# Folding the normalisation's partial sums to 64 rows before the product with ones

## The reference, cut to what matters

```
x = x + 0.5 * ffn(layernorm(x))         # 512 -> 2048 -> 512, weights by their signs, ReLU
x = x + attention(layernorm(x))         # 16 heads of 32
x = x + 0.5 * ffn(layernorm(x))
layernorm(x) = (x - mean(x)) / sqrt(var(x) + 1e-5)      # over the 512 channels
```

## Time and profile before

| | |
|---|---|
| median of 3 runs | 2920.65 us (2915.93 to 2921.74) |
| profiled execution, time | 2917.08 us |
| profiled execution, span | 2915.2 us |
| PE busy | 2864.9 us, 98%, granted clock 0.998 |
| DVE busy | 2049.8 us, 70% |
| ACT busy | 1598.5 us, 55% |
| GpSimd (POOL) busy | 1384.1 us, 47% |

### The profile page before, as it was taken

The page is one execution under the profiler, slowest core; times in us unless marked ns, Lnnn a source line. Parts: engine busy times, 40 slices in busy tenths (PEclk is TensorE's granted clock), DMA queues, the critical chain, the costliest instruction groups (busy, mean ns, idle before and its releaser), DMA issues.

```text
span 2915.2 us, 37959 instructions
## 1 busy us (share of the span) xinstructions
PE 2864.9 (98%) x14288; PEld 1942.2 (67%) x14288; DVE 2049.8 (70%) x3034; ACT 1598.5 (55%) x2847; POOL 1384.1 (47%) x490
## 2 busy tenths in 40 slices
PE   7999999999999999999999999999999999999999
PEld 6888887887755555555555555555555467888887
DVE  5655556768888888888888888888888346555553
ACT  6434434332376766666666666676666653333333
POOL 0000001000089898988888988889888620000000
PEclk9999999999999999999999999999999999999999
DMA  5110102556389999999999999999999852222210
GB/s 188 34 54 29 30 29 66 201 192 191 140 176 189 202 196 202 196 203 194 200 197 202 196 201 195 199 197 204 195 201 209 202 163 58 58 58 58 58 29 29
DMA packets 184375, 424.28 MB, mean 146 GB/s; under 512 B 89728, under 2 KB 90752, under 8 KB 148224
## 3 DMA queue, kind: packets, MB, share of 16 engines
q0 software_dynamic: 31824, 231.75, 38.7%
q1 hardware_dynamic: 152368, 190.11, 23.6%
HBM read 121.91 MB, written 67.63 MB: 65 GB/s over the span
## 4 chain that ended last, share of the span: by engine, by line
PE 90%; DVE 4%; ACT 3%; issue 1%; DMA 1%; POOL 1%; SPq 0%; ACTq 0%; DVEq 0%; POOLq 0%
PE bank L1042 16%; PE bank L1069 16%; PE bank L1038 15%; PE bank L601 15%; PE bank L624 14%; PE bank L751 8%; PE bank L451 3%; ACT att_p L1026 2%; PE bank L1096 1%; POOL att_acc L911 1%; DVE norm_cent L118 1%; ACT head_raw L355 1%; DVE lo L124 0%; PE bank L240 0%; DMA att_dma_acc<-att_p 0%
## 5 line engine op out<-in xcount | busy, mean ns | idle before, releaser
L960 DVE TENSOR_REDUCE att_row_max<-bank 128x1 f32<-128x512 f32 x2048 | 1253.8, 680 | 249.7 <-PE bank L1042 249.6
L1026 ACT ACTIVATE att_p<-bank 128x512 f32<-128x512 f32 x1792 | 910.5, 619 | 399.9 <-PE bank L1038 394.6
L911 POOL TENSOR_TENSOR att_acc<-att_acc,att_p 128x2048 f32<-128x2048 f32 x217 | 1070.8, 4934 | 45.3 <-ACT att_p L1026 41.2
L1042 PE MATMUL bank<-att_k,att_q 96*128 96x512 f32 x2048 | 832.6, 409 | 2.8 <-DVE att_row_max L960 2.6
L1038 PE MATMUL bank<-att_q,att_k 98*128 98x512 f32 x2048 | 818.5, 401 | 9.2 <-ACT att_p L1026 5.3
L1042 PEld LDWEIGHTS bank<-att_k,att_q 96*128 96x128 f32 x2048 | 388.1, 190 | 274.6 <-DVE att_row_max L960 162.1
L1038 PEld LDWEIGHTS bank<-att_q,att_k 98*128 98x128 f32 x2048 | 385.7, 189 | 158.8 <-ACT att_p L1026 44.5
L573 ACT ACTIVATE ffn_hid<-bank,up_s 128x512 f32<-128x512 f32 x256 | 176.2, 688 | 523.1 <-PE bank L601 508.5
L521 DVE TENSOR_TENSOR ffn_hid_lo<-ffn_hid,ffn_hid_hi 128x512 fp32r<-128x512 f32 x256 | 174.6, 687 | 377.8 <-ACT ffn_hid_hi L576 377.8
L1069 PE MATMUL bank<-att_p,att_v 128*32 128x512 f32 x3584 | 439.6, 601 | 0.0
L601 PE MATMUL bank<-hi,ffn_up_w 128*128 128x512 f32 x1024 | 401.1, 392 | 8.9 <-DVE lo L189 4.7
(11 more groups left out here) (117 smaller groups left out, 2390.0 us busy)
## 6 DMA issues: line engine op xcount, KB each, us to landing
att_dma_acc<-att_p POOLq DMA_DIRECT2D x161, 1024.0 KB, 10.3
att_dma_acc<-att_dma_acc POOLq DMA_DIRECT2D x30, 1024.0 KB, 12.6
att_dma_acc<-att_acc POOLq DMA_DIRECT2D x30, 1024.0 KB, 7.4
att_q<-q_hi SPq DMA_DIRECT2D x64, 256.0 KB, 4.0
att_k<-k_hi SPq DMA_DIRECT2D x64, 256.0 KB, 8.1
x<-x_after_ffn SPq DMA_DIRECT2D x15, 1024.0 KB, 7.2
x_after_ffn<-x_out SPq DMA_DIRECT2D x8, 1024.0 KB, 9.5
q_hi<-qkv_o_hi SPq DMA_DIRECT2D x32, 256.0 KB, 2.0
```

The source lines that it names most:

```text
L911: self.nc.gpsimd.tensor_tensor(self.acc[H % 2][:], a[:], self.prob[kt % PR][:], ALU.add).then_inc(self.summed, 1)
L960: self.nc.vector.tensor_reduce(self.row_max[odd][:, qt, q:q + 1], m[:], axis=AX.X, op=ALU.max).then_inc(self.m_read, 1)
L1026: self.nc.scalar.activation(into[:, q * CH:(q + 1) * CH], self.s_ps[(UNITS * H + kt * QC + q) % SR][:], ACT.Exp, scale=SCALE).then_inc(sel ...
L1042: self.nc.tensor.matmul(m[:], self.q_st[T % NB][0:KQ, qt * P:(qt + 1) * P], self.k_st[T % NB][0:KQ, q * CH:(q + 1) * CH], start=True, stop ...
```

## The change

Each statistic's sum is folded once more, from 128 rows to 64, by two further DVE instructions: a copy of rows 64 to 127 of `norm_sum` to rows 0 to 63 of a scratch tile, and an add on 64 rows. Each of the two waits for the instruction before it, through a new semaphore `norm_folding`. The rounded copy of the 64 rows then goes to rows 0 to 63 of one tile `norm_sum_parts`, and what rounding left to rows 64 to 127 of the same tile. PE makes one product of the 128 x 128 matrix of 1/512 with that tile in place of two. The steps, their places in the queues and what PE waits for are as before.

```diff
@@ class Norm, __init__
-        self.sum_hi, self.sum_lo = c.sb("norm_sum_hi", SUM_HI_AT, [P, CH], F32R), c.sb("norm_sum_lo", SUM_LO_AT, [P, CH], F32R)
+        self.parts = c.sb("norm_sum_parts", SUM_HI_AT, [P, CH], F32R)
+        self.folding = c.sem("norm_folding")
@@ centre (the same in square_sums, with 2 * N + 1)
         elif k == 1:
-            ins = nc.vector.tensor_tensor(self.sum[:], self.work[:, 0, :], self.work[:, 1, :], ALU.add)
+            ins = self.fold(dve, 2 * N, 1)
         elif k == 2:
-            ins = nc.vector.tensor_copy(self.sum_hi[:], self.sum[:])
+            ins = self.upper_part()
         elif k == 3:
-            ins = nc.vector.tensor_tensor(self.sum_lo[:], self.sum[:], f32(self.sum_hi[:]), ALU.subtract)
+            ins = self.lower_part()
...
+    def fold(self, dve, which, other):
+        nc, shifted = self.nc, self.work[0:ROWS, 0, :]
+        nc.vector.tensor_tensor(self.sum[:], self.work[:, 0, :], self.work[:, other, :], ALU.add).then_inc(self.folding, 1)
+        dve.wait_ge(self.folding, 2 * which + 1)
+        nc.vector.tensor_copy(shifted, self.sum[ROWS:P, :]).then_inc(self.folding, 1)
+        dve.wait_ge(self.folding, 2 * which + 2)
+        return nc.vector.tensor_tensor(self.sum[0:ROWS, :], self.sum[0:ROWS, :], shifted, ALU.add)
+
+    def upper_part(self):
+        return self.nc.vector.tensor_copy(self.parts[0:ROWS, :], self.sum[0:ROWS, :])
+
+    def lower_part(self):
+        return self.nc.vector.tensor_tensor(self.parts[ROWS:P, :], self.sum[0:ROWS, :], f32(self.parts[0:ROWS, :]), ALU.subtract)
...
@@ vector_first and vector_first_squares: self.fold(dve, 0, 1) and self.fold(dve, 1, 2) in place of the add
@@ tensor
-        nc.tensor.matmul(out[:], self.ones[:], self.sum_hi[:], start=True, stop=False)
-        nc.tensor.matmul(out[:], self.ones[:], self.sum_lo[:], start=False, stop=True).then_inc(self.pe, 1)
+        nc.tensor.matmul(out[:], self.ones[:], self.parts[:], start=True, stop=True).then_inc(self.pe, 1)
```

More of the change, by code:

```diff
@@ L30 @@
 HI1_AT, LO1_AT, X1_AT, CENT_AT, WORK_AT = 128, 136, 144, 152, 160
-SUM_AT, SUM_HI_AT, SUM_LO_AT, VAR_AT = 168, 170, 172, 174
+SUM_AT, SUM_HI_AT, VAR_AT = 168, 170, 174
 HI0_AT, LO0_AT, INV_AT, TMP_AT, HID_AT = 176, 184, 192, 194, 196
@@ L62 @@
 NV, NA = 18, 4
+ROWS = P // 2
 HALF = (slice(0, DT // 2), slice(DT // 2, DT))
@@ L134, in square_sums @@
         if i == 1:
-            ins = nc.vector.tensor_tensor(self.sum[:], self.work[:, 0, :], self.work[:, 1, :], ALU.add)
+            ins = self.fold(dve, 2 * N + 1, 1)
         elif i == 2:
-            ins = nc.vector.tensor_copy(self.sum_hi[:], self.sum[:])
+            ins = self.upper_part()
         elif i == 3:
-            ins = nc.vector.tensor_tensor(self.sum_lo[:], self.sum[:], f32(self.sum_hi[:]), ALU.subtract)
+            ins = self.lower_part()
         ins.then_inc(self.dve, 1)
@@ L179, in vector_first @@
         dve.wait_ge(self.first, 2)
-        nc.vector.tensor_tensor(self.sum[:], work[:, 0, :], work[:, 1, :], ALU.add).then_inc(self.dve, 2)
+        self.fold(dve, 0, 1).then_inc(self.dve, 2)
         for k in (2, 3):
@@ L197, in vector_first_squares @@
         dve.wait_ge(self.first, 6)
-        self.nc.vector.tensor_tensor(self.sum[:], work[:, 0, :], work[:, 2, :], ALU.add).then_inc(self.dve, 2)
+        self.fold(dve, 1, 2).then_inc(self.dve, 2)
         for k in (9, 10):
```

## The result

The kernel after the change takes 2931.4 us (median of 5 runs, 2929.2 to 2935.1) where the kernel before takes 2920.65: ratio 1.0040, with an interval of 1.0028 to 1.0051. So it is slower, by more than the 0.2% that I had set as the bound. I had forecast 2921.0, no measurable change, with 2916 to 2930 as range: direction and range are both missed. Between the medians lie 10.7 us.

A forecast was written before the change was run, and what follows sets the result against it. PE's queue plus its waits was taken as the bound. Costs of 9.4 + 0.9 + 0.8 + 2.4 = 13.5 us less 11.5 saved gave 2.0 us longer, so 2921.0 us from a middle of 2919; range 2916 to 2930.

The forecast's parts named there:

- What bounds the kernel: Whole kernel: PE's queue plus its waits set the time; PE carries 90% of the chain that ended last.
- the nine waits that I started from: PE's waits before a statistic's product: two for a mean, seven for a variance, at 0.0, 9.0, 0.1 and 17.1 to 22.1.
- The fold's price: On DVE at each statistic: the added copy and add cost 1.18 us, 1.46 at the upper bound.
- rival 3: On DVE, the fold's copy costs as much as an add: fold 1.46 us, kernel 6.4 us longer, 2925.4; chance 0.12.
- The removed product: In PE's queue: 0.24 us saved at each of 46 statistics, 0.43 at 9.0, none at 0.0; 11.5 us in all.
- rival 2: Removed product worth less where DMA or ACT re-anchor PE (16.0, 16.1, 13.x): 1.0 us less saving, 2922.0; no separate chance.
- Statistic by statistic: At each of 48 statistics, PE is late by 1.18 us less DVE's lead over PE's product; costs 13.5 us in all.
- The remaining 32: 0 us: At 32 statistics DVE finishes early enough to hide the fold; tightest lead 1.33 us at 10.0, so no cost.
- The sum without the clock: Whole kernel: 13.5 us of costs less 11.5 us of saving, so 2.0 us longer.
- The clock: PE's clock dropping to its lower level after longer waits: counted as 0 us in the sum, kept only as a rival.
- Rival 1: At 0.1 and 17.1 to 22.1, PE idles 2.56 us and its clock falls: 7 x 1.3 = 9.1 us, 2930.1; chance 0.12.
- my own list of signs: Expected in the profile after: among others, matmuls behind waits take 0.50 us if the clock holds, 0.77 and 0.63 if it fell.

The follow-up runs named there:

- the saving alone: The kernel before with one product per statistic, the lower parts computed but not added, so without the fold; ratio 0.9968 to the kernel before.
- before with the product moved: The kernel before with the variance's product of norms 18 to 22, and the steps using it, one tile later; 2912.8 us, ratio 0.9970.
- before with all places moved: The kernel before, without the fold, with products moved to where their sums are ready, and the attention rows' scaling later; 2911.0 us, ratio 0.9966.

## Why the prediction was wrong

- **What bounds the kernel**: right. The list of waits and the timelines carried the argument, and the nine waits that I started from have 11.7 of the 13.7 us by which the waits for a statistic grew.
- **The fold's price**: right. 1.17 to 1.18 us; the copy that changes rows costs 423 ns, like the cast (415). That it might cost an add's time (rival 3) is ruled out.
- **The removed product**: right in its sum, 11.3 us in the trace with the saving alone and 10.7 net in the kernel after, where I had counted 11.5. In most places it is worth 0.29 us, not 0.24 (the spacing of the two starts in the earlier trace rows); at 16.0 and 16.1 it is worth nothing, as rival 2 had it for these two. PE's busy time fell by 3.2 us and not by the 10 that I had expected to see, because the lower clock put 7.4 back.
- **Statistic by statistic**, in waits: 9.0 grew by 6.11 - 4.97 = 1.14 and 17.1 by 1.21, of 1.18 forecast. 0.1 grew by 0.70, of 1.18. At 0.0, which I had put at 0 us, the wait grew by 1.0, but the next one of PE, for DVE's `lo`, is 0.9 shorter. 1.1 grew by 0.66, of 0.86. 10.1 to 13.1 by 0.32 to 0.34 each, of 0.21; the saving of the mean's product brings PE to the variance's earlier, which I had weighed for the 32 others and not for these. In starts PE is 0.46 late there (0.70 - 0.24), which is the 0.21 and the 0.24 of that product. The row maximum between fold and rounding at 14.1 and 15.1 by 1.33 each, of 1.18:

```profile
689.06 0.42 DVE L129 COPY norm_work<-norm_sum 64x512 f32<-64x512 f32 x1
689.52 0.68 DVE L131 TENSOR_TENSOR norm_sum<-norm_sum,norm_work 64x512 f32<-64x512 f32 x1
690.12 0.68 DVE L978 TENSOR_REDUCE att_row_max<-bank 128x1 f32<-128x512 f32 x1
...
690.86 0.50 PE L1060 MATMUL bank<-att_k,att_q 96*128 96x512 f32 x1 [1.59 <-DVE att_row_max L978]
```

- **"The remaining 32: 0 us"**: this step failed for the means 18.0 to 22.0. I looked at whether each product has cover, and it has; but I didn't follow DVE's queue from the mean's fold through the scaling (L431) to the centring. With the slack of 0.71 + 0.30 us gone, PE's wait at the variance is 0.33 us longer than at 17.1, 5 x 0.33 = 1.7 us.
- **The sum without the clock** was 2.0 us and came out as 16.0 - 10.7 = 5.3: the costs were 16.0 instead of 13.5, the saving 10.7 instead of 11.5. With this alone the time would have been 2924.3, within the range, and the forecast of no measurable change would have stood.
- **The clock** is the step that failed, and it decides: the sum holds 0 us for it, and it was 7.4 us in the profiled pair and 8.8 us over the runs of one chip. Rival 1 had about its size (9.1 us, 2930.1), and I gave it 0.12. That the size fits is partly luck: 3.57 - 2.4 is 1.2 us for one fall, not 1.3, a fall really cost 1.4 to 1.6, and not all seven came. Two errors stand in it. I took the clock as a threshold, in which all seven waits fall or none; but at 2.3 to 2.9 us of idle time about half do, so that a loss was near certain and only its size open. And I made a row with 1.88 us without a fall and one of 2.96 us with one into bounds, when the wait of this change, 2.56 to 2.92, was nearer to the second. What I set against it, that PE runs dense ahead of 17.1, doesn't protect: the falls came all the same. The seven waits aren't all of it either: the longer stretch at 9.0 and places without a statistic (664 us, and the attention's end at 2272 us) make up for those of the seven that held. Falls at the attention's end don't need the fold: the traces of three kernels without it (one product, before with the product moved, before with all places moved) have one there too, between 2264 and 2276 us. What brings them, and why the stretch at 9.0 is 6.8 us in some executions and 3.4 in others, isn't settled.
- **The range** ended at 2930; the median is 1.4 us above. With the clock's price counted as half of the waits and the missed 1.7 us, the forecast would have been 2921 + 5 + 2 = 2928, by an estimate in hindsight.

## What to carry to other kernels

A wait for which the bound engine already idles is where an added dependent step costs its full length, and from 2.3 us of idle time on (not at 1.4) PE paid a second time here: the clock fell behind about half of such waits (16 of 31), for 1.4 to 1.6 us each. No sharp limit is shown: at 664 us the clock fell behind 1.79 us too. Whoever moves work from PE to DVE must first ask whether the product can stand later in PE's queue: here that was worth 20 to 21 us, and the fold paid its 6 to 7 us only once it was done at all such places. And cover has to be followed through the queue of the engine that does the new work, to whatever it computes next, not only to the product that takes the result.

## What the runs showed of the hardware that I hadn't expected

**The fall can come after PE has gone on.** PE's timeline of the kernel after at 19.1:

```profile
2554.89 0.50 PE L259 MATMUL bank<-norm_sum_parts,ones_mean 128*128 128x512 f32 x1 [2.91 <-DVE norm_sum_parts L138]
2555.23 0.40 PE L619 MATMUL bank<-hi,ffn_up_w 128*128 128x512 f32 x1
2555.47 0.40 PE L619 MATMUL bank<-lo,ffn_up_w 128*128 128x512 f32 x1
2555.70 0.54 PE L619 MATMUL bank<-hi,ffn_up_w 128*128 128x512 f32 x1
2556.04 0.63 PE L619 MATMUL bank<-lo,ffn_up_w 128*128 128x512 f32 x1
2556.47 0.63 PE L619 MATMUL bank<-hi,ffn_up_w 128*128 128x512 f32 x1
```

The first four matmuls start 0.23 to 0.34 us apart, at 2.4 GHz (granted clock 1.00 up to 2555.7), and only then, 0.9 us behind the wait, the spacing goes to 0.43, at 1.2 GHz (0.50 from 2556.1 on). So to look at the first matmul behind a wait, as my own list of signs did (0.50 if the clock holds, 0.77 if it fell), is not enough: by that sign this wait held. The window behind it is the sign.

**One wait, two outcomes.** 2.59 us at 17.1 held in one execution and fell in the next, and 2.91 to 2.93 us fell in 4 of 10. The page TensorE: Matmul & The Clock Gate of the Trainium skill (What's actually happening) says of a kernel's start that the number of matmuls at the lower clock differs from run to run of the same kernel. The runs here show the like in the middle of a kernel. Its section HAM oscillation tells of waits of about 3 to 5 us, each of which brings the clock down. Here that holds at 3.22 us (6 of 6); at 2.3 to 2.9 us, shorter than the page's waits, 16 of 31 brought it down.

**A copy onto other rows has no price of its own**: 423 ns for rows 64 to 127 onto 0 to 63, float32, against 415 for the cast that stays on its rows.
